# Four image pairs of a deformable layer: from a loop of one block to one block without a loop

## The reference

```python
c3, c5, c7 = jnp.split(x, 3, axis=1)          # 128 channels each
out3, out5, out7 = (deform_block(c, ..., K) for c, K in ((c3, 3), (c5, 5), (c7, 7)))
def deform_block(x, ow, ob, dw, pw, pb, K):
    offsets = conv2d(x, ow, ob, K // 2)        # 2*K*K maps: dy, dx of each tap
    out = deform_depthwise(x, offsets, dw, K, K // 2)  # bilinear samples, weighted per channel
    return conv2d(out, pw, pb, 0)              # 1x1
out = jnp.concatenate([out3, out5, out7], axis=1)
return out * se_weight(out, fc1_w, fc2_w)      # sigmoid gate from mean and max of each channel
```

## Time and profile before

| | |
|---|---|
| median of 3 runs | 6341.27 us (6335.64 to 6345.97) |
| profiled execution, its own time | 6352.18 us |
| its span in the trace | 6350.4 us, 121429 instructions |
| PE busy | 5693.4 us, 90% |
| DVE busy | 4855.1 us, 76% |
| ACT busy | 3901.0 us, 61% |
| POOL busy | 663.3 us, 10% |
| layer 1, its four pairs | from 1993.4 to 5355.6 us |
| its block behind the loop | from 5357.3 to about 5385 us |

### The profile page before, as it was taken

How to read it: one execution, slowest core, us unless ns; L and a number is a source line. 1 busy time by engine, 2 the same in 40 slices (tenths; PEclk the granted TensorE clock), 3 DMA queues, 4 the chain that set the end, 5 groups by cost and what they waited for, 6 DMA issues and landing times. The chain is left out here.

```text
span 6350.4 us, 121429 instructions
## 1 busy us (share of the span) xinstructions
PE 5693.4 (90%) x45900; PEld 3982.8 (63%) x45900; DVE 4855.1 (76%) x10150; ACT 3901.0 (61%) x5362; POOL 663.3 (10%) x802
## 2 busy tenths in 40 slices
PE   5999999999968988999989989899998997899798
PEld 2455554555434557885568865688755786555688
DVE  5888888888865789887799977898878988343333
ACT  3777766777652557885578855688755886121242
POOL 2111211111102001011010010110001100000000
PEclk9999999999988999999999999999999998999898
DMA  4212221222114544555455554555454554111698
GB/s 146 66 55 56 64 59 43 65 67 60 39 54 113 123 117 112 129 119 123 108 124 122 123 129 109 120 123 122 109 135 110 125 123 118 66 60 40 156 235 200
DMA packets 197671, 661.96 MB, mean 104 GB/s; under 512 B 62985, under 2 KB 64833, under 8 KB 154243
## 3 DMA queue, kind: packets, MB, share of 16 engines
q1 hardware_dynamic: 172723, 603.24, 38.6%
q0 software_dynamic: 24320, 50.37, 3.2%
HBM read 540.04 MB, written 62.71 MB: 95 GB/s over the span
## 5 line engine op out<-in xcount | busy, mean ns | idle before, releaser
L2428 PE MATMUL b_near_p<-b_near_work,b_near_hkt 64*128 64x144 f32 (+37 forms) x27520 | 2118.5, 309 | 257.1 <-DVE b_near_acc L2302 161.6
L2428 PEld LDWEIGHTS b_near_p<-b_near_work,b_near_hkt 64*128 64x128 f32 x27520 | 1969.5, 195 | 469.0 <-DVE b_near_work L2373 286.9
L2373 DVE TENSOR_TENSOR b_near_work<-b_near_work 128x140 f32<-128x140 f32 (+26 forms) x5312 | 1610.7, 354 | 218.8 <-PE b_near_p L2428 133.7
L2273 ACT ACTIVATE b_near_work<-b_near_work,b_near_mcol 128x512 f32<-128x512 f32 (+6 forms) x1328 | 765.1, 647 | 860.5 <-DVE b_near_work L2373 779.6
L2277 ACT ACTIVATE b_near_work<-b_near_work,b_near_mrow 128x544 f32<-128x544 f32 (+6 forms) x1328 | 762.5, 646 | 0.0
L539 ACT ACTIVATE a_ex<-a_p_t 128x1024 f32<-128x1024 f32 x512 | 524.2, 1024 | 365.2 <-PE a_p_t L477 364.1
L614 DVE TENSOR_REDUCE a_nm<-a_p_x 128x1 f16<-128x1024 f32 x512 | 625.6, 1222 | 154.5 <-PE a_p_x L466 147.7
L2302 DVE SCALAR_TENSOR_TENSOR b_near_acc<-b_near_p,b_near_dwc,b_near_acc 128x323 f32<-128x323 f32 (+14 forms) x1088 | 622.1, 574 | 157.4 <-PE b_near_p L2428 155.8
L1812 PE MATMUL b_near_p<-b_near_hp,b_near_ow 128*98 128x480 f32 (+14 forms) x1568 | 658.2, 570 | 0.0
L620 DVE TENSOR_TENSOR a_el<-a_ex,a_eh 128x1024 f16<-128x1024 f32 x512 | 621.7, 1214 | 8.0 <-ACT a_eh L544 6.9
L544 ACT CAST a_eh<-a_ex 128x1024 f16<-128x1024 f32 x512 | 535.4, 1046 | 50.8
(11 more groups left out here) (225 smaller groups left out, 5635.2 us busy)
## 6 DMA issues: line engine op xcount, KB each, us to landing
b_near_work<-sampling_positions_near SPq DMA_DIRECT2D x666, 512.0 KB, 6.5
d_win<-merged_kernels SPq DMA_DIRECT2D x192, 263.0 KB, 6.7
b_near_xin<-x SPq DMA_DIRECT2D x24, 1024.0 KB, 8.2
a_xr<-in_x SPq DMA_DIRECT2D x12, 1536.0 KB, 6.4
a_xh<-in_x SPq DMA_DIRECT2D x9, 1536.0 KB, 6.5
x<-a_xr SPq DMA_DIRECT2D x9, 1536.0 KB, 5.7
b_near_xr<-x SPq DMA_DIRECT2D x13, 1024.0 KB, 15.9
x<-b_near_xr SPq DMA_DIRECT2D x13, 1024.0 KB, 4.7
```

What stands on the lines that cost most here:

```text
L2273: last = e.activation(rx[:, u, xo[c]:xo[c + 1]].rearrange("p (a b) -> p a b", a=H), pp[:, b, 1, :].rearrange("p (a b) -> p a b", a=H)[:, : ...
L2373: e.tensor_tensor(S[:, k % NS, 0:(r1 - r0) * w].rearrange("p (a b) -> p a b", b=w), rx[:, u, xo[cc]:xo[cc + 1]].rearrange("p (a b) -> p a ...
L2428: last = e.matmul(G[:, a0 - top:z0 - top, c0 - left:c1 - left], hkt[64 * s:64 * s + 64, SIDE * cr + cc, :], S[64 * s:64 * s + 64, k % NS, ...
```

## The change

It has five parts.
1. Without `far` the four pairs are written out one behind another in one block: `pr` is a Python number. The loop and the meeting of the engines between pairs are gone.
2. All waits are on constants, and `tick(e)` emits its increment with `far` only.
3. The first stage of pairs 1 to 3 is now a stage that follows another (`follows`): its first position reads, its first hats and its first sums wait on semaphores of the stage before, and so do two things that the end of the block stood for: SP's load of x at tap 1 and DVE's copy of the norm parameters wait for `s_hp` (the last image padded by POOL). `turn` alternates the two hat buffers over the boundary.
4. The last stage of the last pair (`final`) has no convolutions, nothing of theirs on DVE, POOL and SP, no loads of x and no read of following positions.
5. Each stage clears the ten tap semaphores of the next one; before, the first stage cleared twenty and the third ten. The closing block doesn't wait for loads that are no longer made.

```diff
+        def tick(e):
+            if far:
+                e.sem_inc(sh["tick"], 1)
...
             e.wait_ge(s_red.sem, s_red.at(q + 1))
-            e.sem_inc(sh["tick"], 1)
+            tick(e)
...
@@ stage_of
+            follows = g > 0 if far else g > 0 or pr > 0
+            final = not far and g == 2 and pr == B // 2 - 1
+            turn = g if far else g + pr
...
-            convs = CONV_UNITS[g]
+            convs = [] if final else CONV_UNITS[g]
+            conv_at, evac, over, store = ({}, {}, {}, {}) if final else (plan.at, plan.evac, plan.over, plan.store)
...
@@ sync
-                if g == 0:
-                    for sem in (*taps[1].all, *taps[2].all):
-                        e.sem_clear(sem.sem)
+                for sem in taps[nxt].all:
+                    e.sem_clear(sem.sem)
...
-                        elif g > 0:
-                            e.wait_ge(prev.s_ab.sem, prev.s_ab.at(2 * (last_in_slot(g - 1, b) + 1)))
+                        elif follows:
+                            e.wait_ge(prev.s_ab.sem, prev.s_ab.at(2 * (last_in_slot(gp, b) + 1)))
                         read_positions(e, pp, g, tap, tp.s_pp[b])
...
-                    if tap == 1:
+                    if tap == 1 and not final:
+                        if g == 0 and follows:
+                            e.wait_ge(s_hp.sem, s_hp.at(pr * 6 + 6))
...
-                e.wait_ge(tp.s_ab.sem, tp.s_ab.at(2 * (last_in_slot(g, RING_AT[nxt]) + 1)))
-                if g == 2:
-                    for sem in taps[0].all:
-                        e.sem_clear(sem.sem)
-                ahead = taps[nxt].s_pp[RING_AT[nxt]]
-                read_positions(e, pp, nxt, 0, ahead)
-                if far or g == 2:
-                    e.wait_ge(ahead.sem, ahead.at(32))
+                if not final:
+                    e.wait_ge(tp.s_ab.sem, tp.s_ab.at(2 * (last_in_slot(g, RING_AT[nxt]) + 1)))
+                    ahead = taps[nxt].s_pp[RING_AT[nxt]]
+                    read_positions(e, pp, nxt, 0, ahead)
+                    if far:
+                        e.wait_ge(ahead.sem, ahead.at(32))
...
@@ gpsimd
+                if final:
+                    return
...
@@ vector
                 if g == 0:
+                    if follows:
+                        e.wait_ge(s_hp.sem, s_hp.at(pr * 6 + 6))
                     e.tensor_copy(gnp[:, :, 0:2, :], sh["gn"][:, :, ds(now, 2), :])
...
@@ tensor
-                if g > 0:
-                    e.wait_ge(prev.s_g.sem, prev.s_g.at(sums_of(g - 1)))
+                if follows:
+                    e.wait_ge(prev.s_g.sem, prev.s_g.at(sums_of(gp)))
                 sums_in_taps(e, gp)
...
-        with nc.Fori(0, B // 2) as pr:
-            stages = [stage_of(pr, g) for g in range(G3)]
-            if far:
+        if far:
+            with nc.Fori(0, B // 2) as pr:
+                stages = [stage_of(pr, g) for g in range(G3)]
...
+        else:
+            stages = [stage_of(pr, g) for pr in range(B // 2) for g in range(G3)]
+            with nc.Block() as block:
...
+                @block.tensor
+                def _(e):
+                    for stage in stages:
+                        stage[4](e)
...
-                e.wait_ge(s_x.sem, s_x.at(16 * (5 * pe + 3)))
-                e.wait_ge(s_row.sem, s_row.at(16 * (3 * pe + 2)))
-                e.wait_ge(ahead.sem, ahead.at(32))
+                if far:
+                    e.wait_ge(s_x.sem, s_x.at(16 * (5 * pe + 3)))
+                    e.wait_ge(s_row.sem, s_row.at(16 * (3 * pe + 2)))
+                    e.wait_ge(ahead.sem, ahead.at(32))
```

More of the change, by code:

```diff
@@ L2200, in sync @@
                         store_result(e, pr, 0, before)
-                    if tap in plan.store:
-                        c = plan.store[tap]
+                    if tap in store:
+                        c = store[tap]
                         store_positions(e, *convs[c], q_of(c), ring_of(c)[1])
@@ L2207, in sync @@
                             e.wait_ge(s_hp.sem, s_hp.at(pr * 6 + 10))
-                            e.sem_inc(sh["tick"], 1)
+                            tick(e)
                             load_x(e, 2, after)
-                    if g == 2 and tap == 8:
+                    if g == 2 and tap == 8 and not final:
                         e.wait_ge(s_hp.sem, s_hp.at(pr * 6 + 8))
-                        e.sem_inc(sh["tick"], 1)
+                        tick(e)
                         e.wait_ge(s_h8.sem, s_h8.at(pr * 3 + 4))
-                        e.sem_inc(sh["tick"], 1)
+                        tick(e)
                         load_x(e, 1, after)
@@ L2316, in beside @@
                         e.wait_ge(s_pe.sem, s_pe.at(stage * 4 + 2 * s + 2))
-                        e.sem_inc(sh["tick"], 1)
+                        tick(e)
                         largest(e, gp, s)
-                    if k in plan.evac:
-                        c = plan.evac[k]
+                    if k in evac:
+                        c = evac[k]
                         take_offsets(e, *convs[c], conv_u[c], *ring_of(c), pr * 8 + 8 + c)
-                    if k in plan.over:
-                        gj = plan.over[k]
+                    if k in over:
+                        gj = over[k]
                         excess(e, gj, q_of(convs.index((gj, 3))), job_of(gj))
@@ L2346, in beside @@
                             decide(e, 2, job_of(2))
-                        for tap, c in plan.store.items():
+                        for tap, c in store.items():
                             if convs[c][1] == 3 and k == (tap + 2) * ITEMS1:
@@ L2358, in vector @@
                 for tap in range(TAPS):
-                    u = (tap + g) % 2
+                    u = (tap + turn) % 2
                     (rows, yo), (cols, xo) = tap_spans(K, tap)
@@ L2465, in layer1, with _ @@
                         clear(nc, [s_far["ld"].sem])
[L2467 to L2493 removed]
+        else:
+            stages = [stage_of(pr, g) for pr in range(B // 2) for g in range(G3)]
+            with nc.Block() as block:
+                @block.sync
+                def _(e):
+                    for stage in stages:
+                        stage[0](e)
+                @block.gpsimd
+                def _(e):
+                    for stage in stages:
+                        stage[1](e)
+                @block.scalar
+                def _(e):
+                    for stage in stages:
+                        stage[2](e)
+                @block.vector
+                def _(e):
+                    for stage in stages:
+                        stage[3](e)
+                @block.tensor
+                def _(e):
+                    for stage in stages:
+                        stage[4](e)
         with nc.Block() as block:
[L2496 removed]
+            left = 0 if far else len(CONV_UNITS[2])
+            last_u = [((B // 2) * UNITS1 + P0.u0 + c - left, b, (B // 2) * USES[b] + p - left // 2) for c, (b, p) in enumerate(zip(P0.bank, P0.prior))]
             pe, last_b = B // 2, B - 2
```

69 lines of the change are left out of this document (23 added, 46 removed).

## The result

The changed kernel takes **6234.68 us** (median of 4 runs, 6225.70 to 6243.62) where the kernel before took 6343.35 us beside it: ratio 0.9831, interval [0.9815, 0.9847], 108.7 us less. Run again beside other kernels, it took 6230.33 us against 6343.36 (0.9819 [0.9796, 0.9842]), 113.0 us less. The direction was right, some 30 us were missing from the sum.

What follows compares the result with a forecast made beforehand. No engine is full: pair boundaries stall, and in the last stage PE limits taps with convolutions, ACT those without. 58 + 19 + 3 = 80 us off the median 6341.3 gives 6261 us, range 6242 to 6288.

Steps and rivals of the forecast that it cites:

- The last stage: Last K = 7 stage of the last pair: without convolutions it runs at ACT's pace, 58 us less (45.5 to 60.3).
- All of POOL's work in the stage: Last K = 7 stage: POOL's work there listed among what the change removes, with no gain of its own priced.
- The loop's end: Where pairs meet: from last product to hats of tap 1 8.3 us instead of 14.66; 19 us for three (6 to 21).
- Constants and ticks: DVE's dependent steps in all pairs: 0.12 us each, 8.6 us in all, a third taken, 3 us less (0 to 8.6).
- registers cost more: Rival: registers cost more than dependent steps show, on PE's and SP's queues too; 15 us more gain, 6246 us; chance 0.08.
- The Trainium skill's rule: DVE's semaphores: one after each of eight copies costs nothing extra; by it the constants term is 0, the sum 77 us.
- taps kept 7.58 us: Rival, last K = 7 stage: free taps find another limit, 7.97 us each, 6274 us; chance 0.22 shared with the stall rival.
- no wait took the stall's place: Rival, pair boundaries: the stall becomes a wait for positions or sums, 6274 us; chance 0.22 shared with the taps rival.
- fresh code: Rival, written-out pairs 1 to 3: new instruction packets stall by 0.5 us each, 114 us, ending at 6375 us; chance 0.03.

Runs made afterwards that it cites:

- e3_convs: The changed kernel with convolutions, loads and the read ahead kept in the last pair; 6287.29 us, ratio 0.9905 to the kernel before.
- b2_grid_dve: The kernel before, with the last K = 5 grid addition in the K = 7 stages done by DVE instead of POOL; 6345.66 us, ratio 0.9998.
- e10_pool_kept: The changed kernel, but the last pair still loads x and POOL still normalises and pads it, without convolutions; 6245.85 us.
- e12_dve_late: The changed kernel with five tiny DVE reductions added before `excess` for K = 5, near tap 39 of K = 7 in pairs 0 to 2; 6244.91 us.
- e1_ticks: The changed kernel with the tick increments back on all engines, waits still on constants; 6245.65 us, ratio 0.9826 to the kernel before.
- e5_ticks_dve: The changed kernel with tick increments back on DVE alone; 6234.64 us.
- e6_ticks_rest: The changed kernel with tick increments back on all engines but DVE; 6240.95 us.
- e11_later_pad: The kernel of `e9_subtract_dve` with POOL's first cast and subtraction moved behind its copies into the following K = 7 stage; 6219.34 us, ratio 0.9795.
- e9_subtract_dve: The changed kernel with the second subtraction of padded halves in K = 7 of pairs 0 to 2 done by DVE instead of POOL; 6221.73 us, ratio 0.9804.
- a0_after: The changed kernel run again unchanged, as base for later runs; 6230.33 us.

## Why the forecast was right in direction and 30 us short

- **The last stage: right in size, partly for another reason.** 60.2 us against 58. Its taps and ACT's pace came as forecast. But with convolutions and nothing else undone (`e3_convs`) the stage takes 433.4 us, so they are worth 52.7. The other 7.4 us were in no term of mine. Tap by tap, the kernel before has 3.3 of them from tap 40 on (2.3 went in `b2_grid_dve`), 1.5 at the taps with `take_offsets`, and 1.8 at two taps near tap 16, where two profiles of the changed kernel differ by as much.
- **POOL's work was costed in the wrong stage: the first step that failed.** "All of POOL's work in the stage" went at nothing, hidden inside the last K = 7 stage. It runs ahead, into the end of K = 5, and there holds DVE: 8.5 us, of which `e10_pool_kept` gave back 6.4 (of two single profiles; at least 3).
- **The loop's end: right mechanism, 21 for 19 us** by the hats of tap 1, as the two copies hide. The term ended too early: the K = 3 stages behind it are 2.4 us a pair shorter too, more than half of it because a late DVE meets POOL's clearing. The 3.8 us of pair 0, also beside the clearing, had no term at all.
- **Constants and ticks: the second step that failed.** "I count 0.12 us" for each dependent step and take a third: 3 us. The 0.12 is right. The third is too little: where PE is said to cover the steps they come nearly in full, 1.5 us in each K = 7 stage. And wrong above all is that a step is worth its length at the most. In `e12_dve_late` a third of a microsecond decides whether DVE is held beside POOL, and with the hold TensorE's clock always halved: the change takes off 3 us a stage at taps 40 and 41, for a shift of 0.34 us on DVE and 0.15 on POOL. Ticks alone (`e1_ticks`, `e5_ticks_dve`, `e6_ticks_rest`) showed nothing in the whole time that can be told from scatter, and no hold near tap 40. The rival "registers cost more" (6246) was the nearest in size, but put the cost on the queues of PE and SP.
- **The Trainium skill's rule** (VectorE: DVE Perf Modes, section The DRAIN you can't avoid) made this term 0. The pace of the dependent steps did change (in `excess`, with ticks and constants in `e1_ticks`, they start 0.29 us apart, in the changed kernel 0.18), so the rule doesn't hold for them; but most of what counted lay outside the rule and outside my sum.
- **The other rivals** didn't come: taps kept 7.58 us, no wait took the stall's place, fresh code costs nothing (383 instruction packets in all, no stall in pairs 1 to 3).

Open stays the 5 us in the K = 5 stages of pairs 0 to 2, which scatter by 5 us each between profiles of one program; in the second profile of the changed kernel they are no shorter than before. Over all profiles the 12 K = 5 stages of the loop take 292.3 us on average (289.6 to 292.8), the 35 written out with all of POOL's work 290.2 (284.4 to 293.5), so some 2 us a stage look real; only 0.24 of them are the taps with `take_offsets`. Open is also whether the register counts or the loop itself move DVE and POOL together near tap 40. Taking the ticks out of the loop was not tried, nor register counts without a loop.

## What to carry to other kernels

Busy time of the same instructions that differs between two kernels or two stages (here 229.6 against 235.9 us of DVE) can be the trace of one engine that holds another: list DVE's long outliers beside POOL's instructions before pricing a change. Price a shift of one engine against POOL not by its length but by what overlaps afterwards, and count behind it the low clock that a starved PE gets. Work placed on POOL "for nothing" can be paid by DVE. Moved to a place where DVE waits anyway it costs little: in `e11_later_pad` cast and subtraction hold DVE's products in the K = 7 stage (16 of them take 10.7 us), and these stages are no longer for it (434.3 to 437.0 us against 434.4 to 437.8 in `e9_subtract_dve`).

## What the runs showed of the hardware that I had not expected

- POOL's TENSOR_TENSOR (2.16 us) and CAST (1.1 us) stop DVE's products until they end: 6.01 for 2.23 us, 1.09 for 0.42. Its MEMSET (1.80 us) stops turned rows, 2.19 for 0.50 us, and no product. Beside its TENSOR_SCALAR of 8.3 us for two most products keep their length, and some, as some turned rows, take 0.85 us more.
- TensorE's granted clock fell to 1.2 GHz behind a stretch in which PE was busy for 1.74 of 4 us, and stood there for 8 us of nearly full work. Hold and clock together cost 1.9 us at each of two taps; where the clock fell without a hold (`a0_after`, pair 2) the tap took 9.01 instead of 7.51 us.
- One program gives stages that differ by 1.5 to 5 us from run to run, in steps at a few fixed taps; single stages are compared safely only over several profiles, single taps much more closely.
